# Two self-attention stages: the projection of a later group and the quotient move ahead of the last score units, the exp units are ordered by heads, and block 0 of the maxima takes one mask product

## The reference, cut to what matters

```
q = split_heads(hidden_states @ Wq.T + bq)      # 16 heads of 32
k = split_heads(hidden_states @ Wk.T + bk)
v = split_heads(hidden_states @ Wv.T + bv)
scores = jnp.einsum('bhqd,bhkd->bhqk', q, k) * scale
scores = jnp.where(causal, scores, jnp.float32(-jnp.inf))
attn = jax.nn.softmax(scores, axis=-1)
out = jnp.einsum('bhqk,bhkd->bhqd', attn, v)
out = out.transpose(0, 2, 1, 3).reshape(B, S, HIDDEN)
return out @ Wo.T + bo
```

## Time and profile before

| | us |
|---|---|
| median of 3 runs | 3143.84 |
| lowest and highest run | 3139.68 and 3151.02 |
| profiled execution | 3156.45 |
| its span | 3154.7 |
| first self-attention stage, from the first S unit | 60.5 to 549 of the span |
| second one | 1684 to 2171 of the span |

### The profile page before, as it was taken

How to read it: one execution, slowest core, us unless ns; L and a number is a source line. 1 busy time by engine, 2 the same in 40 slices (tenths; PEclk the granted TensorE clock), 3 DMA queues, 4 the chain that set the end, 5 groups by cost and what they waited for, 6 DMA issues and landing times. The chain is left out here.

```text
span 3154.7 us, 35002 instructions
## 1 busy us (share of the span) xinstructions
PE 2211.2 (70%) x12378; PEld 1507.4 (48%) x12410; DVE 1897.6 (60%) x3060; ACT 1173.2 (37%) x2000; POOL 527.9 (17%) x498
## 2 busy tenths in 40 slices
PE   6999997578788328888848999995001638777770
PEld 5777775222222115555427777772001627655550
DVE  3355555578778556666653455554888343488876
ACT  2222221266666423333322222221785112255550
POOL 1112122101011000000001112211000040266654
PEclk7798998699999669999966889897555569999995
DMA  4222120521321210000012212210000200399875
GB/s 127 68 61 61 41 61 21 129 64 36 78 63 37 107 67 0 0 0 0 0 61 60 61 41 61 61 41 15 0 0 0 96 1 0 129 305 303 300 240 160
DMA packets 79911, 233.25 MB, mean 74 GB/s; under 512 B 16688, under 2 KB 17968, under 8 KB 70960
## 3 DMA queue, kind: packets, MB, share of 16 engines
q0 software_dynamic: 23552, 121.67, 12.9%
q1 hardware_dynamic: 55216, 109.70, 12.4%
q10 hardware_dynamic: 1024, 0.26, 0.0%
HBM read 149.23 MB, written 31.50 MB: 57 GB/s over the span
## 5 line engine op out<-in xcount | busy, mean ns | idle before, releaser
L773 DVE TENSOR_REDUCE x_negm<-x_M 128x2 f32<-128x1024 f32 x256 | 309.0, 1224 | 78.8 <-PE x_M L833 78.0
L307 ACT ACTIVATE L_attn_PT<-L_attn_T 128x512 f32<-128x512 f32 x320 | 179.2, 596 | 461.9 <-PE L_attn_T L499 461.8
L729 ACT ACTIVATE x_PT<-x_T 128x512 f32<-128x512 f32 x512 | 278.5, 598 | 185.2 <-PE x_T L853 179.9
L375 DVE TENSOR_REDUCE L_attn_negm<-L_attn_M 128x2 f32<-128x1024 f32 (+1 forms) x192 | 195.4, 1044 | 169.5 <-PE L_attn_M L480 169.0
L478 PE MATMUL L_attn_M<-L_attn_QKS 96*128 96x256 f32 (+3 forms) x512 | 195.5, 439 | 49.6 <-DMA L_attn_QKS<-L_attn_HL 27.4
L497 PE MATMUL L_attn_T<-L_attn_QKS 97*128 97x384 f32 (+3 forms) x512 | 193.2, 436 | 12.5 <-DMA L_attn_QKS<-L_attn_mT 10.5
L853 PE MATMUL x_T<-x_QS,x_KS 49*128 49x512 f32 x512 | 137.1, 532 | 46.7 <-ACT x_PT L729 41.6
L1310 PE MATMUL graph_P<-ident,graph_L 128*128 128x128 f32 x64 | 15.7, 427 | 214.0 <-DVE graph_L L1383 208.7
L221 POOL DMA_DIRECT2D L_attn_QKS<-L_attn_HL x64 | 34.8, 543 | 747.5 <-DVE L_attn_mT L379 669.0
L478 PEld LDWEIGHTS L_attn_M<-L_attn_QKS 96*128 96x128 f32 x512 | 123.4, 241 | 71.7 <-DVE L_attn_negm L375 15.1
L862 PE MATMUL x_O<-x_PT,x_V 128*32 128x512 f32 x1024 | 150.3, 662 | 8.3 <-issue 8.3
(11 more groups left out here) (365 smaller groups left out, 5462.6 us busy)
## 6 DMA issues: line engine op xcount, KB each, us to landing
L_attn_QKS<-L_attn_HL SPq DMA_DIRECT2D x192, 128.0 KB, 4.8
L_attn_QKS<-L_attn_HL POOLq DMA_DIRECT2D x192, 128.0 KB, 3.7
moe_y_rows<-slots_YS SPq DMA_DIRECT2D x48, 256.0 KB
x_QS<-x_xh SPq DMA_DIRECT2D x128, 64.0 KB
X<-in_x SPq DMA_DIRECT2D x4, 1024.0 KB
x_xh<-x_XTH SPq DMA_DIRECT2D x4, 1024.0 KB, 3.9
x_xl<-x_XTL SPq DMA_DIRECT2D x4, 1024.0 KB, 5.1
x_KS<-x_ch SPq DMA_DIRECT2D x32, 128.0 KB, 4.5
```

The lines of the kernel that those rows point to most:

```text
L307: ac.activation(PT[:, s, bank], T[:, bank], ACT.Exp, scale=SCALE).then_inc(t_free, 1)
L375: last = ve.tensor_reduce(negm[:, g % 2, h0:h0 + nh, i], src, AX.X, ALU.max, negate=True)
L729: ac.activation(PT[:, s // 4, head(s), :], T[(STEPS_S * g + s) % 3][:], ACT.Exp, scale=SCALE).then_inc(t_free, 1)
L773: ve.tensor_reduce(negm[:, g % 2, u // 4:4:2, u % 4], m[:].rearrange("p (r k) -> p r k", r=2), AX.X, ALU.max, negate=True).then_inc(m_free, 1)
```

## The change

The projection of group n + 2 and the quotient of group n - 1 move from behind S 4 to just behind S 2, so that maxima 4, S 3, maxima 5 and S 4 come behind them. The S units are ordered so that the first three hold all that heads 0 and 1 need, and `stack` waits for each head by itself, not for the whole group. ScalarE takes the q half as soon as its bank is full. ScalarE's part of the quotient moves from Q to R. Unit 5 of the maxima gets one mask product over the four blocks in place of four. P's parts follow the new order of the S units. The moments of the layer norm take 8 steps in each R instead of 12 in the first three batches, and POOL applies the norm one group later in the program.

```diff
-            plan += maxima(0, 1) + [("S", n, 1)] + maxima(2, 3) + [("S", n, 2)] + maxima(4)
-            plan += [("S", n, 3)] + maxima(5) + [("S", n, 4)]
+            plan += maxima(0, 1) + [("S", n, 1)] + maxima(2, 3) + [("S", n, 2)]
             plan += [("Q", n - 1)] if n else []
             plan += [("M", "qk", n + 2)] if n + 2 < GROUPS else []
+            plan += maxima(4) + [("S", n, 3)] + maxima(5) + [("S", n, 4)]
...
-        EXP_UNITS = [[(0, 0, 0), (1, 0, 512)], [(2, 0, 0), (3, 0, 512)],
+        EXP_UNITS = [[(0, 0, 0), (1, 0, 512)],
                      [(0, 1, 0), (0, 3, 384), (1, 1, 512), (1, 3, 896)],
-                     [(2, 1, 0), (2, 3, 384), (3, 1, 512), (3, 3, 896)],
-                     [(h, 2, 256 * h) for h in range(4)]]
+                     [(h, 2, 256 * h) for h in range(4)],
+                     [(2, 0, 0), (3, 0, 512)],
+                     [(2, 1, 0), (2, 3, 384), (3, 1, 512), (3, 3, 896)]]
...
-            queue.wait_ge(m_free, drained("qk", n))
-            if n >= 2:
-                queue.wait_ge(t_full, 2 * 5 * (n - 1))
             for h in heads:
                 rows = slice(HD * h, HD * h + HD)
                 arrived = stacked[r][h]
+                queue.wait_ge(qk_hi, 2 * n + 2)
+                if n >= 2:
+                    queue.wait_ge(t_full, 2 * (5 * (n - 2) + UNITS_OF[h]))
                 queue.dma_start(QKS[0:HD, r, :, h, :].bitcast(F32), HL[rows, 1:3, :].bitcast(F32)).then_inc(arrived, 16)
+                queue.wait_ge(m_free, drained("qk", n))
...
-                    act.wait_ge(m_full, at["qk", n] + 1)
+                    act.wait_ge(q_full, n + 1)
...
-                elif x[0] == "Q":
+                elif x[0] == "R":
...
-                    for _ in range(12):
+                    for _ in range(8 if n < GROUPS - G else 12):
...
-                        for h, i, c in MAX_UNITS[u]:
+                        if u == 5:
+                            pe.matmul(m[:, 0:BANK], C["identr"][:], mask_rows, start=True, stop=False)
+                            for h, i, c in MAX_UNITS[u]:
+                                last = pe.matmul(m[:, c:c + P], QKS[0:R, r, 0, h, 0:P], QKS[0:R, r, 1, h, 0:P],
+                                                 start=False, stop=(h == 3))
+                        for h, i, c in MAX_UNITS[u] if u < 5 else ():
```

More of the change, by code:

```diff
@@ L197, in stage_self_attention @@
         at = {(x[1], x[2]): n for n, x in enumerate(m_units)}
-        hi_at = {(x[1], x[2]): n for n, x in enumerate(x for x in m_units if x[1] in ("xt", "qk"))}
+        hi_at = {x[2]: n for n, x in enumerate(x for x in m_units if x[1] == "xt")}
         drained = lambda kind, arg: at[kind, arg] + 3
@@ L204, in stage_self_attention @@
                      [(h, 1, 256 * h) for h in range(4)], [(h, 0, 128 * h) for h in range(4)]]
-        EXP_UNITS = [[(0, 0, 0), (1, 0, 512)], [(2, 0, 0), (3, 0, 512)],
+        EXP_UNITS = [[(0, 0, 0), (1, 0, 512)],
                      [(0, 1, 0), (0, 3, 384), (1, 1, 512), (1, 3, 896)],
-                     [(2, 1, 0), (2, 3, 384), (3, 1, 512), (3, 3, 896)],
-                     [(h, 2, 256 * h) for h in range(4)]]
-        PV_PARTS = [(0,), (1, 3), (2,)]
-        EXP_READER = [0, 0, 1, 1, 2]
+                     [(h, 2, 256 * h) for h in range(4)],
+                     [(2, 0, 0), (3, 0, 512)],
+                     [(2, 1, 0), (2, 3, 384), (3, 1, 512), (3, 3, 896)]]
+        UNITS_OF = [3, 3, 5, 5]
+        PV_PARTS = [(0,), (2,), (1, 3)]
+        PV_NEEDS = [4, 4, 5]
+        EXP_READER = [0, 2, 1, 0, 2]
         PT_AT = {(h, j): (u, c) for u, unit in enumerate(EXP_UNITS) for h, j, c in unit}
@@ L250, in _, with apply_norm @@
             pool.wait_ge(b_in, 32)
+            def apply_norm(b):
+                pool.wait_ge(residual, NT * (b + 1))
+                pool.wait_ge(moments, MOMENTS * (b + 1))
+                for i in range(NT):
+                    gp.tensor_scalar(X[:, b, i, :], X[:, b, i, :], ln["mean"][:, i:i + 1], ln["rstd"][:, i:i + 1],
+                                     ALU.subtract, ALU.mult).then_inc(applied, 1)
             stack(pool, 0, (1, 3))
@@ L260, in _ @@
                         gp.tensor_tensor(X[:, b, i, :], X[:, b, i, :], BR[:, 1, :], ALU.add).then_inc(residual, 1)
-                if g == 3 and b >= 1:
-                    pool.wait_ge(residual, NT * b)
-                    pool.wait_ge(moments, MOMENTS * b)
-                    for i in range(NT):
-                        gp.tensor_scalar(X[:, b - 1, i, :], X[:, b - 1, i, :], ln["mean"][:, i:i + 1], ln["rstd"][:, i:i + 1],
-                                         ALU.subtract, ALU.mult).then_inc(applied, 1)
+                if g == 0 and b >= 2:
+                    apply_norm(b - 2)
+            apply_norm(NB - 2)
         @block.scalar
@@ L290, in _ @@
                             act.wait_ge(arrived, 16 * 3 * ((n - 1) // 2 + 1))
-                    ac.activation(HL[:, 1, :], src[:, 0:BANK], ACT.Identity, bias=BQK[:, 0, c:c + 1])
-                    ac.activation(HL[:, 2, :], src[:, BANK:], ACT.Identity, bias=BQK[:, 1, c:c + 1]).then_inc(hi_done, 1)
+                    ac.activation(HL[:, 1, :], src[:, 0:BANK], ACT.Identity, bias=BQK[:, 0, c:c + 1]).then_inc(qk_hi, 1)
+                    act.wait_ge(m_full, at["qk", n] + 1)
+                    ac.activation(HL[:, 2, :], src[:, BANK:], ACT.Identity, bias=BQK[:, 1, c:c + 1]).then_inc(qk_hi, 1)
                 elif x[0] == "M" and x[1] == "mt":
@@ L343, in _ @@
                     m = M[n % 2]
-                    dve.wait_ge(m_full, n + 1)
+                    if kind != "qk":
+                        dve.wait_ge(m_full, n + 1)
                     if kind == "qk" and arg == 0:
                         dve.wait_ge(b_in, 32)
-                    if kind in ("xt", "qk"):
-                        dve.wait_ge(hi_done, hi_at[kind, arg] + 1)
                     if kind == "xt":
+                        dve.wait_ge(hi_done, hi_at[arg] + 1)
                         ks = slice(2 * arg[1], 2 * arg[1] + 2)
@@ L426, in _ @@
             second = lambda hi, lo, a: lo if a == 2 else hi
+            mask_rows = C["mask_qk"][:].unsqueeze(1).to_broadcast([P, NT, P])
             for x in plan:
@@ L469, in _ @@
                                            lambda a, k: second(XTH, XTL, a)[:, k, :])
+                            if w == 0:
+                                last.then_inc(q_full, 1)
                     elif kind == "max":
@@ L508, in _ @@
                             t.wait_ge(m_free, drained("v", (b, g // 2, 1)))
-                    t.wait_ge(t_free, 2 + 2 * (5 * n + (2, 4, 5)[part]))
+                    t.wait_ge(t_free, 2 + 2 * (5 * n + PV_NEEDS[part]))
                     for j in PV_PARTS[part]:
@@ L517, in _ @@
                                 last = pe.matmul(out[HD * h:HD * (h + 1), P * j:S], lhs, PT[:, u, c:c + w],
-                                                 start=(j == 0), stop=(part == 2))
+                                                 start=(j == 0), stop=(j == 3))
                     last.then_inc(pv_part, 1)
```

4 lines of the change are left out of this document (3 added, 1 removed).

## The result

The changed kernel takes 3036.23 us in the median of 4 runs (3024.42 to 3040.38), the kernel before 3147.43 us in its 4 (3139.68 to 3179.95). The ratio is 0.9625, 95% interval 0.9578 to 0.9672, which is 118 us or 3.7% faster; the two medians lie 111 us apart. The forecast was 3055 us, 88.6 us less than before.

The account below looks back on a forecast made before the run. TensorE was taken as the bound, with its waits and its granted clock (0.86) to gain. 30.7 + 34.9 + 23 + 7 + 1 - 8 = 88.6 us off 3143.84 gave 3055 us; whole range 3020 to 3105.

Parts of the forecast that it names:

- What the forecast named as signs: In the changed profile: no HL waits, full turns about 22.3 us at clock 1.00, SP's first DMA 1 us after the projection.
- Waits, 30.7 us: TensorE's waits for HL (27.3 us) and the row of turned maxima (3.4 us) all go; between 20 and 30.7 us.
- Clock of the five turns, 34.9 us: Turns n = 1, 7, 12 (first stage), 1, 11 (second) lose low stretches begun at HL waits; 0 to 34.9 us.
- Clock of the six turned-input turns, 17 us: Turns n = 2, 6, 10 keep their fall, but the earlier projection brings the clock back sooner; 17 us saved.
- First turns, 6.2 us: Each stage's first turn runs at the low level until its projection, now earlier; 3.1 us saved in each.
- the early q half ahead of the loop, 1 us: One high part less in VectorE's chain that holds up maxima 1, in each stage; 1 us, from 0 to 3.
- The mask, 7 us: One 512-wide mask matmul in maxima 5 saves 0.23 us in each of 32 groups; 7 us, from 0 to 12.
- New waits on VectorE, minus 8 us: Turning of the maxima waits for VectorE's reductions, 0.3 us in each of 28 turns; 8 us lost, from 0 to 28.
- The q half early, in the loop nothing of its own: In the loop, the gain of taking the q half early was counted as contained in the earlier DMAs.
- the third rival: TensorE waits for VectorE before maxima 5 and the turning, the clock falling each time; 3160 us, chance 0.05.
- The clock did not stay low as often: Rival: HL waits go but low stretches come anyway, so only 31 us are saved; 3113 us, chance 0.12.
- The transfers did land earlier: Rival it answers: HL transfers land no earlier, volume alone setting landing; 22 us saved, 3122 us, chance 0.04.

Follow-up runs that it names:

- e7: The kernel before with nothing but the one mask product in maxima 5; ratio to the kernel before 0.9953.
- e1: The changed kernel with its four mask products in maxima 5 put back; ratio to the kernel before 0.9661.
- e2: The changed kernel with projection and quotient back behind the last S unit, all else kept; ratio to the kernel before 0.9780.
- e3: The kernel before with only the new place of projection and quotient in the plan; ratio to the kernel before 0.9963.
- e10: The changed kernel with ScalarE taking the q half only when both banks are full; ratio to the kernel before 0.9716.
- e11: The changed kernel with the q half taken only when both banks are full and ScalarE's quotient part back at Q; ratio to the kernel before 0.9742.
- e6: The changed kernel with all twelve DMAs of a group issued from SP's queue; ratio to the kernel before 0.9664.
- e4: The changed kernel with the DMAs of all heads waiting for the whole group and the low parts again; ratio to the kernel before 0.9714.

## Why the prediction was right, and where its sizes were off

The mechanism held. Every wait for HL and for the row of turned maxima left the turns, and the low stretches that began at such waits went with them. What the forecast named as signs came: SP's first issue 0.8 us behind the end of the last product (about 1 expected), the fourth behind the last S unit, full turns at clock 1.00 (21.99 us, expected 22.3).

*Waits, 30.7 us.* All of it came, and somewhat more. The turns that had only waits and no low stretch became 18.5 us shorter where 15.7 were forecast. The record of idle time understates a wait: it shows 16.3 us in these nine turns, and the mask and the new waits nearly cancel, so some 0.3 us a turn with two waits stood in no row. In the earlier trace rows the S unit ahead of the wait of 0.96 us took 1.76 us from start to start, and takes 0.64 where no wait follows: the wait cost 1.12.

*Clock of the five turns, 34.9 us.* With their waits they give 50.6 us, 49.6 forecast: right.

*Clock of the six turned-input turns, 17 us.* This is the step that was mis-sized, and the largest single error, 10 us: the forecast took 6.8 us at the low level out of five of them and half of that out of the sixth, 37 us in sum. Measured, they had 6.8, 10.2 and 6.8 us in the first stage and 0, 6.8 and 10.2 in the second, 41 us where before it were 99: 58 x 0.46 = 27 us. What the forecast took for granted is that the fall comes where it came before. In the five turns that fell, the clock came back 2.1 to 4.3 us into the projection, as forecast; but it fell 0.4 and 0.6 us after the second wait in the two turns with 10.2 us, 1.3 to 1.6 us after it in the three with 6.8, and not at all in the sixth. The rate itself was exact. Three turns of the changed kernel have the same instructions and differ in their low time only: 28.82 us with none, 31.96 with 6.83, 33.54 with 10.24, which is 0.46 us for each us both times.

*First turns, 6.2 us, and the early q half ahead of the loop, 1 us.* 17.0 us less at the low level in both together (30.7 to 20.5 and 27.3 to 20.5), 7.8 us at 0.46. The wait ahead of the loop fell from 2.23 to 0.92 us, 1.3 in each stage and not 0.5.

*The mask, 7 us.* 0.22 us for the product (e7), as worked out, but 0.15 us of a turn (e1): 5 us.

*New waits on VectorE, minus 8 us.* 0.23 us a turn by e2, with 0.3 forecast. The view of waits shows none of it; it lies in S 3 (0.84 us from start to start, 0.69 in e2), maxima 5 (0.73 and 0.68) and S 4 (1.09 and 1.02).

*The q half early, in the loop nothing of its own.* Here the total was right and the credit wrong. The forecast took the order for the source of the gain. By e3 the order alone brings next to nothing, by e2 all the rest without the order brings 2.2 of some 3.7%, and by e10 and e11 it is the pace of the conversions that keeps maxima 5 from waiting: 0.65 us a turn, 18 us in 28 turns, for the one line on ScalarE (e10's turns took 14.6 us more from the first P to the last, with fewer falls in the turned-input turns). The chain of VectorE in the forecast had this in it, but not that its absence would bring the third rival.

*The rivals.* The clock did not stay low as often: the low stretches of the five turns are gone, and of the six turned-input turns 41 of 99 us are left. The transfers did land earlier. "DMA: Bandwidth & Descriptors" of the Trainium skill, section "Issuing engines are not separate DMA queues", says that queues of several issuers share the 16 engines; e6 agrees in so far as one queue did as well as two. That volume alone sets the landing was the forecast's own reading of it, and here it didn't bind. "TensorE: Matmul & The Clock Gate" of the Trainium skill, section "What's actually happening", has the gate run in a rhythm of its own; 0, 6.8 and 10.2 us at the low level behind the same waits of the same program fit that. Why a given one of the six turns falls for that long is not settled by these runs.

## What to carry to other kernels

Before moving work of the engine that bounds a kernel to an earlier place, follow what must be drained behind it up to the next user of its buffer: the move is worth only what that chain leaves (e3: nearly nothing), and one semaphore placed a bank earlier was worth 0.65 us in each turn of 22 (e10). Where a kernel has a clock that falls, price short waits by the low stretch behind them, and place work with a long drain ahead of long unbroken work that needs nothing from it (here the turned input ahead of P, 23 us). Read turns from start to start beside the view of waits, since a wait of some tenths doesn't show there.

## What the runs showed of the hardware

- The granted clock stayed at 1.00 in turns with one wait of 0.64 us (e10, e11: 24 turns of 22.6 us, no low stretch), and fell behind 18 of 26 waits of 0.96 us in e3, in n = 4, 7, 8, 11 and others with no second wait in the turn. Before, pairs of waits of about 1.0 and 0.7 us like that of the earlier trace rows brought no fall in nine turns and one in n = 12 (0.96 and 0.72 us); n = 7 and n = 11 of the second stage fell with a longer wait in the pair (1.52 and 2.11). In e7 the pairs of n = 3, 7 and 11 brought falls (1.07 and 0.74 us in n = 11) and that of n = 4 did not (1.07 and 0.75). So it is no matter of the idle time alone, and what decides it stays open.
- Twelve DMAs of HL into QKS from one queue took 8.9 us to issue, eleven at about 0.6 us and one at 1.56 (e6). Where SP and POOL issue six each at the same time, SP's sixth took 2.12 us in the earlier trace rows and 2.01 us in e4, and its six took 7.3 and 7.1 us. So two queues at once saved SP under 2 us for a whole set, and four of its six issues took longer (0.9 to 2.1 us).
